# Gelu in place in the PSUM bank, with the high and low halves of each hidden chunk made from that bank

## What is computed

```
x = x + xattn(layernorm(x), ctx, ctx, mask, ...)      # one head of width 16, tiled to 256, context of 64 rows
x = x + ffn(layernorm(x), w1, b1, w2, b2)

ffn:  h   = gelu(x @ binarize(w1).T + b1)             # 1024 hidden columns
      out = h @ binarize(w2).T + b2
binarize(w) = mean(|w|, axis=1) * sign(w)
```

## Time and profile before

| | |
|---|---|
| time, three runs | 441.08, 441.1 and 450.6 us, median 441.1 |
| span of the profiled execution | 438.1 us |
| DVE busy | 369.6 us, 84% |
| PE busy | 346.5 us, 79% |
| POOL busy | 283.8 us, 65% |
| ACT busy | 259.1 us, 59% |
| h_lo, line 647 | 128 instructions, 164.2 us, mean 1312 ns |
| gelu, line 496 | 128 instructions, 94.5 us, mean 777 ns |

### The profile page before, as it was taken

One profiled execution on the slowest core, in us unless ns is written; L12 is line 12 of the kernel. 1 busy time (PEld: TensorE's weight loads), 2 busy tenths in 40 slices (PEclk: granted clock), 3 DMA queues, 4 the chain that ended last, 5 costly groups with the idle time before them and its releaser, 6 DMA issues. The chain is left out here.

```text
span 438.1 us, 7839 instructions
## 1 busy us (share of the span) xinstructions
PE 346.5 (79%) x2381; PEld 234.1 (53%) x2381; DVE 369.6 (84%) x718; ACT 259.1 (59%) x486; POOL 283.8 (65%) x368
## 2 busy tenths in 40 slices
PE   6777507989796969787888978787979796969693
PEld 4433404667565645556564737464646564546462
DVE  2949427999989899999898998989998999997756
ACT  1258107768493858576584857574848493847460
POOL 1400334858686786868686868686968687783824
PEclk9965566999899999999898999998989999998998
DMA  8600100101111111110201011111111111010102
GB/s 265 234 0 6 45 0 1 49 1 49 49 49 49 51 48 48 48 48 21 75 0 70 26 55 41 48 48 48 48 48 48 48 48 48 0 48 1 48 2 96
DMA packets 9424, 21.39 MB, mean 49 GB/s; under 512 B 1720, under 2 KB 4928, under 8 KB 9408
## 3 DMA queue, kind: packets, MB, share of 16 engines
q1 hardware_dynamic: 8496, 21.14, 13.4%
q10 hardware_dynamic: 912, 0.05, 0.1%
HBM read 12.80 MB, written 8.39 MB: 48 GB/s over the span
## 5 line engine op out<-in xcount | busy, mean ns | idle before, releaser
L647 DVE SCALAR_TENSOR_TENSOR h_lo<-h_sb,h_scale,h_hi 128x512 f16<-128x512 f32 x128 | 164.2, 1312 | 12.2 <-POOL h_hi L415 7.2
L1185 PE MATMUL psZ<-sgn2T,h_hi 128*128 128x256 f16 x512 | 120.4, 279 | 45.0 <-DVE h_lo L647 44.6
L1185 PE MATMUL psZ<-sgn2T,h_lo 128*128 128x256 f16 x512 | 120.6, 280 | 0.0
L1171 PE MATMUL psY<-x_hi,sgn1T 128*128 128x512 f16 x256 | 100.3, 392 | 1.6 <-ACT sgn1T L619 1.6
L496 ACT ACTIVATE h_sb<-psY,b_col,alpha1x 128x512 f32<-128x512 f32 x128 | 94.5, 777 | 9.4 <-PE psY L1171 7.1
L1171 PE MATMUL psY<-x_lo,sgn1T 128*128 128x512 f16 x256 | 99.8, 390 | 0.0
L1185 PEld LDWEIGHTS psZ<-sgn2T,h_hi 128*128 128x128 f16 x512 | 50.9, 99 | 65.1 <-DVE h_lo L647 56.6
L386 POOL TENSOR_SCALAR vare<-st 128x4 f32<-128x4 f32 x32 | 12.9, 402 | 89.1 <-DVE st L639 64.1
L415 POOL TENSOR_SCALAR h_hi<-h_sb,h_scale 128x512 f16<-128x512 f32 x64 | 47.1, 740 | 30.2 <-PE psZ L1185 18.8
L400 POOL TENSOR_SCALAR xh<-x,rstd,nmr 128x256 f32<-128x256 f32 x64 | 59.6, 943 | 3.4 <-issue 1.9
L1121 PE MATMUL psW<-ident,xh 128*128 128x128 f32 x256 | 36.2, 287 | 28.8 <-POOL xh L400 28.8
(11 more groups left out here) (141 smaller groups left out, 525.0 us busy)
## 6 DMA issues: line engine op xcount, KB each, us to landing
x_in<-in_x SPq DMA_DIRECT2D x16, 512.0 KB, 3.3
out_x<-z_sb SPq DMA_DIRECT2D x15, 512.0 KB, 2.6
w_sb<-in_L_ffn_w SPq DMA_DIRECT2D x2, 1024.0 KB, 9.9
ctx_sb<-in_ctx SPq DMA_DIRECT2D x1, 1024.0 KB, 7.5
out_x<-z_sb SPq DMA_DIRECT2D x2, 256.0 KB, 2.1
wk_sb<-in_L_xattn_Wk SPq DMA_DIRECT2D x1, 256.0 KB, 3.1
wq_sb<-in_L_xattn_Wq SPq DMA_DIRECT2D x1, 256.0 KB, 3.4
wv_sb<-in_L_xattn_Wv SPq DMA_DIRECT2D x1, 256.0 KB, 7.6
```

The lines of the kernel that those rows point to most:

```text
L647: nc.vector.scalar_tensor_tensor(out=h_lo[c % 4][:, :], in0=h_sb[c % 4][:, :], scalar=h_scale[:, :], in1=h_hi[c % 4][:, :], op0=ALU.mult, ...
L1171: last = nc.tensor.matmul(psY[c % 4][:, :], sgn1T[:, k, c * P:(c + 1) * P], part[slot][:, k, :], start=(n == 0), stop=(n == 2 * KD - 1))
L1185: last = nc.tensor.matmul(psZ[j // 2][:, (j % 2) * D:(j % 2 + 1) * D], part[c % 4][:, j * P:(j + 1) * P], sgn2T[:, c, :], start=(c == 0 an ...
```

## The change

Gelu writes its result back into the PSUM bank that it reads. h_sb is gone. ACT makes all eight h_hi, each right after its gelu, and DVE all eight h_lo; both read the bank. POOL makes none. A bank is free for chunk c+4 only when h_lo has read it, so first_product(c) waits for h_lo_done and not for gelu_done. Two orders change: on DVE h_lo 1 moves ahead of xT_lo, and in body 0 copy_signs_2 moves behind h_lo 2 and 3.

```diff
     def hi(i, par, c):                                  # POOL: removed with its four calls
-        wait(pool, z_added, val(i, par, C, c - 3))
-        wait_apart(pool, gelu_done, val(i, par, C, c + 1))
-        nc.gpsimd.tensor_scalar(h_hi[c % 4][:, :], h_sb[c % 4][:, :], h_scale[:, :], 1.0,
-                                ALU.mult, ALU.mult).then_inc(hi_by_pool, 1)
     def gelu(i, par, c):                                # ACT
         wait(act, y_ready, val(i, par, C, c + 1))
-        wait(act, h_lo_done, val(i, par, C, c - 3))
-        nc.scalar.activation(h_sb[c % 4][:, :], psY[c % 4][:, :], ACT.Gelu,
+        nc.scalar.activation(psY[c % 4][:, :], psY[c % 4][:, :], ACT.Gelu,
                              bias=b1_col[:, c:c + 1], scale=alpha1x[:, c:c + 1]) \
             .then_inc(gelu_done, 1)
     def hi(i, par, c):                                  # ACT
         wait(act, gelu_done, val(i, par, C, c + 1))
         wait(act, z_added, val(i, par, C, c - 3))
-        nc.scalar.activation(h_hi[c % 4][:, :], h_sb[c % 4][:, :], ACT.Copy,
-                             scale=h_scale[:, :]).then_inc(hi_by_act, 1)
+        nc.scalar.activation(h_hi[c % 4][:, :], psY[c % 4][:, :], ACT.Copy,
+                             scale=h_scale[:, :]).then_inc(h_hi_done, 1)
     # ACT, body
-            gelu(i, par, 0)
-            hi(i, par, 0)
-            gelu(i, par, 1)
-            gelu(i, par, 2)
-            gelu(i, par, 3)
+            for c in range(4):
+                gelu(i, par, c)
+                hi(i, par, c)
...
-            gelu(i, par, 4)
-            hi(i, par, 2)
-            hi(i, par, 3)
-            gelu(i, par, 5)
-            hi(i, par, 4)
-            gelu(i, par, 6)
-            gelu(i, par, 7)
+            for c in range(4, C):
+                gelu(i, par, c)
+                hi(i, par, c)
     def lo(i, par, c):                                  # DVE
-        owner, chunks = (hi_by_act, ACT_HI) if c in ACT_HI else (hi_by_pool, POOL_HI)
-        wait(dve, owner, val(i, par, len(chunks), chunks.index(c) + 1))
-        nc.vector.scalar_tensor_tensor(out=h_lo[c % 4][:, :], in0=h_sb[c % 4][:, :],
+        wait(dve, h_hi_done, val(i, par, C, c + 1))
+        nc.vector.scalar_tensor_tensor(out=h_lo[c % 4][:, :], in0=psY[c % 4][:, :],
     # DVE, body
         if ffn:
             lo(i, par, 0)
+            lo(i, par, 1)
...
         if early:
             split_xT(i, par + 2)
-        if is_body(i, par, 0):
-            copy_signs_2()
         if is_body(i, par, -1):
             signs(sgn1, neg1, w1_flat, 1, sgn1_ready)
         if ffn:
-            lo(i, par, 1)
             lo(i, par, 2)
             lo(i, par, 3)
+        if is_body(i, par, 0):
+            copy_signs_2()
     def first_product(i, par, c):                       # PE
-        wait(pe, gelu_done, val(i, par, C, c - 3))
+        wait(pe, h_lo_done, val(i, par, C, c - 3))
```

More of the change, by code:

```diff
@@ L62, in xattn_ffn_kernel @@
     V_AT = 32
-    POOL_HI = (1, 5, 6, 7)
-    ACT_HI = (0, 2, 3, 4)
     TAIL = 2
@@ L167, in xattn_ffn_kernel @@
         x_lo = [sb(f"x_lo{n}", [P, KD, S], F16) for n in range(2)]
-        h_sb = [sb(f"h_sb{n}", [P, S]) for n in range(4)]
         h_hi = [sb(f"h_hi{n}", [P, S], F16) for n in range(4)]
@@ L258, in xattn_ffn_kernel @@
         gelu_done = sem("gelu_done")
-        hi_by_act = sem("hi_by_act")
-        hi_by_pool = sem("hi_by_pool")
+        h_hi_done = sem("h_hi_done")
         h_lo_done = sem("h_lo_done")
@@ L408, in top_of_hidden @@
                                                bass.bass_isa.ReduceOp.max).then_inc(top_reduced, 1)
-            def hi(i, par, c):
-                wait(pool, z_added, val(i, par, C, c - 3))
-                wait_apart(pool, gelu_done, val(i, par, C, c + 1))
-                nc.gpsimd.tensor_scalar(h_hi[c % 4][:, :], h_sb[c % 4][:, :], h_scale[:, :], 1.0,
-                                        ALU.mult, ALU.mult).then_inc(hi_by_pool, 1)
             def body(i, par):
-                if is_body(i, par, 0):
-                    pool.wait_ge(scales_ready, 1)
                 if has(i, par + 2) and not is_body(i, par, -1):
                     norm(i, par + 2, 0, x_in[par % 2])
-                if has(i, par):
-                    hi(i, par, 1)
                 if has(i, par + 1):
                     norm(i, par + 1, 1, x1)
[L427 to L430, removed]
                 if has(i, par - 1):
```

## The result

The changed kernel takes 501.0 us in the median, against 442.75 us for the kernel before in the same runs: a ratio of 1.135, 95% interval 1.130 to 1.139. Some executions show a lower granted clock and a longer time (here one of the four of the kernel before, 450.6 us, and further down one of the four of early_lo, 579.7 us at 0.56); the ratios and intervals leave them out, the medians of all executions do not. The changed kernel is slower, as forecast, but 32 us above the forecast of 469 and 8 above the end of the range. Its profiled execution has a span of 498.7 us, 60.6 more than before.

What follows compares the result with a forecast made beforehand. DVE was taken to bound the kernel; with the change, waits for the held PSUM banks make each body +2.0 us. Fourteen bodies add 28 us to the 438.1 us span, 466.1, plus 3.0 to the median: 469 us, range 448 to 493.

Steps and rivals of the forecast that it cites:

- The block of h_lo: DVE's h_lo 6 and 7 stand blocked beside POOL's TENSOR_TENSOR; reading PSUM gives back about 4.0 us a body.
- The prices: Instruction times taken from similar rows: h_lo from PSUM 0.74 us, h_hi 683 ns, gelu into PSUM 0.78 us.
- The walk: One body followed from x1 to the next x1 through the engines' waits: 24.95 us against 22.94, +2.0 us.
- Both holds of the order: first_product(4) to (7) wait for h_lo 0 to 3; on ACT h_hi 4 to 7 wait for second products 0 to 3.
- PE's first stall: PE idle ahead of first_product(4) until h_lo 0 is done, 2.3 us a body.
- The ends at 0: First body, last body and the halves at the ends of the kernel were left at 0 in the sum.
- about +1: First body, where copy_signs_2 stands ahead of second_product(0): about +1 us, left out of the sum.
- the -2 for the last: Last body, without exp and x_hi: h_lo 6 and 7 lose their block, about -2 us, left out.
- the clock: Rival: granted clock falls in every body behind PE's gaps, slow stretch on the path, 14 x 1.6 = +22, 491 us; chance 0.18.
- The argument against the rival: In the earlier trace the next body had PE gaps too and kept a clock of 1.00.
- DVE's lateness: DVE's slack in the kernel before, said to hide most of the 1.6 us lost in a body at clock 0.93.
- The range: 448 to 493 us, from the upper end of "nothing much" to the clock case, leaving out about 2 in 10.

Runs made afterwards that it cites:

- early_lo: lo_first with h_lo 0 and 1 also moved, ahead of x1's statistics on DVE; 420.2 us.
- pool_small: The kernel before, with POOL's two long additions and DVE's last add cut to one column of each 256; 381.7 us, ratio 0.865.
- warm: The changed kernel with ten extra unread matmuls ahead of first_product(4) and ten ahead of first_product(6) in the loop bodies; 472.6 us, ratio 1.070.
- lo_first_warm: lo_first with ten extra unread matmuls ahead of first_product(4) in the loop bodies; 436.2 us.
- lo_first: The changed kernel with h_lo 2 and 3 moved ahead of xT_lo in DVE's order; 455.0 us, ratio 1.030.
- buf8: The changed kernel with eight buffers each for h_hi and h_lo where it had four; 465.8 us.
- sbuf_h: The changed kernel with gelu writing to h_sb in SBUF again, h_hi and h_lo reading it, first_product waiting for gelu; 445.2 us, ratio 1.009.
- warm_first: The changed kernel with ten extra unread matmuls ahead of first_product(4) only; 483.4 us, ratio 1.093.
- warm_second: The changed kernel with ten extra unread matmuls ahead of first_product(6) only; 478.5 us, ratio 1.082.

## Why the forecast was right in kind and too low

- **The block of h_lo, -4.0 us a body:** right. pool_small gave 3.8, and the changed kernel has no h_lo over 752 ns. POOL's four xh fell from 4.13 to 2.17 us.
- **The prices:** h_lo 742 ns as taken, h_hi 687 (683), gelu into PSUM 746 against 777, inside its bounds. The Trainium skill's "ScalarE: Activation LUTs", section "Step-by-step: what each stage is for", is right in direction: 31 ns an instruction, which here is nothing.
- **The walk, +2.0 us a body:** right. 24.92 in warm against 24.95; 22.51 in lo_first_warm against 22.6. Both holds of the order are shown singly, by lo_first and buf8. Two smaller things were off: PE's first stall is 3.02 us and not 2.3, and 22.94 us, from two neighbouring bodies, is a little low for the kernel before, whose 12 distances from x1 to x1 between 97.92 and 374.70 have a mean of 23.07.
- **The ends at 0:** mis-sized. From x1 of body 0 to that of body 1 it is 105.88 - 76.76 = 29.1 us, where before it was 97.92 - 76.35 = 21.6: 7.5 us more, against the 3.0 that "about +1" on top of 2.0 makes. Its granted clock is 0.88, as in the bodies with two slow stretches, where before it was 1.00; how much that makes I did not test apart. From x1 of body 14 to the end it is 39.8 against 39.9 us. In warm, at a clock of 0.99, the same piece takes 470.5 - 432.26 = 38.2 us, so most of the -2 for the last came, and a slow stretch took it back.
- **The step that failed is the clock.** I had it as a rival with 0.18, at one slow stretch a body, 491 us, and at nothing in the sum. It happened in every body of the loop, and in about every second one twice. From 105.88 to 431.92 seven distances from x1 to x1 are 26.6 us and five are 27.9 to 28.0; their mean is 27.17 against 24.92 at full clock, 2.25 us a body and 27.0 us in all. The next distance, 26.97 us, is 23.86 in warm: 3.1 more. So 30 us of the 32 between 469 and 501 are shown to be the clock; the other pieces nearly cancel, which is luck: the first body adds 5.5 us over the 2.0 that the sum had for it, and the 13 behind it stay 3.3 below theirs at full clock. The argument against the rival, that the next body of the earlier trace rows had gaps too and kept its clock, was a sample of two. What it did show was a fall in one body of two, behind gaps of 1.3 and 1.7 us. With longer gaps, now 3.02 and 2.23, and work of PE's path directly behind them, the fall had to be taken as the likeliest case, with the price of a stretch at half clock in full: in the kernel before, bodies with one slow stretch take some 23.3 us and those without 22.5 to 22.9, so DVE's lateness had hidden the greater part.
- **The range** took its upper end from one stretch a body; two stretches in about every second body were not in any case.

## What to carry to other kernels

Writing a result back into its accumulator bank doesn't add work, it adds a hold: find the last reader of the bank in its own engine's order, and everything that stands ahead of it there. The same two instructions two places earlier were worth 46 us, and the second ring, h_hi's four buffers, 35 in the changed kernel and 20 in early_lo. Where such a hold makes PE wait in the middle of its path, price what runs behind the gap at half clock, once for each gap, and take that as a likely case: here it happened behind such gaps in half of the bodies or in all of them. And compare bodies of the same granted clock before giving a difference another cause: in sbuf_h 1.4 us a body look like the block and are the clock.

## What the runs showed of the hardware

- At one long PE gap, of 2.23 us in warm_first and of 3.0 to 3.2 us in warm_second, the granted clock fell to 0.50 in about every second body; in lo_first, with a gap as long as that of warm_second, in every body. So the length of the gap alone doesn't say whether it falls. A slow stretch cost 1.4 to 1.7 us where the work behind it was on the path. Matmuls whose result nobody reads gained 28 us by keeping the clock.
- DVE's COPY_PREDICATED of two SBUF tensors is also held up beside POOL's TENSOR_TENSOR: 2.59 us in sbuf_h, against 0.44 in the changed kernel, where POOL is idle at that time. By the Trainium skill, "SBUF — State Buffer", section "Who interferes with whom", a DVE instruction with two SBUF inputs contends with POOL instructions that read SBUF; the trace agrees.
- POOL's x1b takes 2.60 us beside a blocked h_lo and 2.34 in the changed kernel.
